# First attention layer: the twelfth tile's probabilities summed on TensorE instead of VectorE, and the keys' last third made one pair of tiles later

## The reference, cut to what matters

```python
def _L0_xattn_ref(hidden_q, kv_c, Wq, w_kc_q, w_kc_kv, W_qr, W_kr, Wo):
    q_hk = (hidden_q @ Wq.T).reshape(Bv, Sv, H, K)
    q_big = _apply_rope(jnp.einsum('bshk,hkq->bshq', q_hk, w_kc_q), ...)
    kv_r = _apply_rope(kv_c, sin_k[None], cos_k[None])
    q_r = jnp.einsum('bshq,hqr->bhsr', q_big, W_qr)
    k_r = jnp.einsum('bld,hdr->bhlr', kv_r, W_kr)
    scores = jnp.einsum('bhsr,bhlr->bhsl', q_r, k_r)
    attn = jax.nn.softmax(scores, axis=-1)
    ctx_c = jnp.einsum('bhsl,bld->bhsd', attn, kv_r)
    ...
x = x + _L0_xattn_ref(_layernorm(x, axis=-1), ctx_512, ...)
```

## Time and profile before

| | |
|---|---|
| median of three runs | 3072.91 us (3068.79 to 3073.55) |
| profiled execution | 3062.97 us, its span 3061.2 us, mean granted clock 0.944 |
| busy in the span | PE 2756.9 us (90%), DVE 1929.9 (63%), ACT 1131.7 (37%), POOL 1876.1 (61%) |
| first layer's attention | about 110 to 1425 us in the span |
| POOL's additions there, L1183 | 608 instructions, 804.8 us |
| DVE's `context`, L1325, in 180 to 1420 us | 28 with a `prob` operand, 51.9 us busy, 56.3 us of waiting for POOL ahead of them |

### The profile page before, as it was taken

The page is one execution under the profiler, slowest core; times in us unless marked ns, Lnnn a source line. Parts: engine busy times, 40 slices in busy tenths (PEclk is TensorE's granted clock), DMA queues, the critical chain, the costliest instruction groups (busy, mean ns, idle before and its releaser), DMA issues. The chain is left out here.

```text
span 3061.2 us, 43235 instructions
## 1 busy us (share of the span) xinstructions
PE 2756.9 (90%) x15928; PEld 1710.1 (56%) x15928; DVE 1929.9 (63%) x2342; ACT 1131.7 (37%) x1640; POOL 1876.1 (61%) x1239
## 2 busy tenths in 40 slices
PE   7688989989899989998789979999999999987898
PEld 6444545545445545454678855555555555545665
DVE  3576657665766666663666556665665765646664
ACT  3124441444134432443433224443444443433331
POOL 0469975999769976995200007877877877951111
PEclk8789999999999999999899988999999999997999
DMA  8333331333213331331000033323323323310000
GB/s 298 113 79 78 88 98 35 71 93 91 66 41 91 97 85 35 75 88 63 32 1 1 1 78 80 86 61 83 86 61 83 86 68 79 86 42 13 7 7 12
DMA packets 98841, 209.19 MB, mean 68 GB/s; under 512 B 30306, under 2 KB 74322, under 8 KB 91116
## 3 DMA queue, kind: packets, MB, share of 16 engines
q1 hardware_dynamic: 98636, 206.44, 26.4%
HBM read 135.36 MB, written 46.00 MB: 59 GB/s over the span
## 5 line engine op out<-in xcount | busy, mean ns | idle before, releaser
L1289 DVE TENSOR_REDUCE maxpart<-pair 112x2 f32<-112x1000 f32 x744 | 890.2, 1197 | 428.3 <-PE pair L978 427.2
L1118 ACT ACTIVATE prob<-wide 125x896 f32<-125x896 f32 x768 | 671.5, 918 | 723.0 <-PE wide L1004 619.8
L1183 POOL TENSOR_TENSOR sums<-sums,prob 125x448 f32<-125x448 f32 x544 | 708.6, 1324 | 45.9 <-POOL sums L1183 38.6
L1018 PE MATMUL single<-prob,kv 125*64 125x448 f32 x3072 | 692.1, 565 | 0.7 <-ACT prob L1118 0.7
L1186 POOL TENSOR_TENSOR sums<-sums,prob 125x896 f32<-125x896 f32 x284 | 615.0, 2165 | 113.4 <-ACT prob L1118 76.9
L999 PE MATMUL wide<-qhigh,kparts 64*125 64x448 f32 x3072 | 447.8, 369 | 1.8 <-ACT prob L1118 1.4
L978 PE MATMUL pair<-kparts,qhigh 64*112 64x500 f32 x1488 | 340.7, 454 | 82.0 <-DVE maxpart L1289 80.7
L1018 PEld LDWEIGHTS single<-prob,kv 125*64 125x64 f32 x3072 | 215.5, 139 | 264.2 <-issue 196.8
L978 PEld LDWEIGHTS pair<-kparts,qhigh 64*112 64x112 f32 x1488 | 131.6, 173 | 379.9 <-DVE maxpart L1289 244.1
L999 PEld LDWEIGHTS wide<-qhigh,kparts 64*125 64x125 f32 x3072 | 285.2, 185 | 60.0 <-issue 29.1
L1004 PE MATMUL wide<-shift,ones_row 64*125 64x448 f32 x1536 | 283.1, 364 | 0.5 <-DMA shift<-maxrow 0.5
(11 more groups left out here) (334 smaller groups left out, 4033.3 us busy)
## 6 DMA issues: line engine op xcount, KB each, us to landing
kparts<-keys_merged SPq DMA_DIRECT2D x64, 750.0 KB, 8.8
kparts<-kparts SPq DMA_DIRECT2D x96, 250.0 KB, 3.1
keys_merged<-kparts SPq DMA_DIRECT2D x32, 750.0 KB, 10.4
recip<-zrec_merged SPq DMA_DIRECT2D x124, 112.0 KB, 2.8
w_low_values<-w_merged SPq DMA_DIRECT2D x64, 192.0 KB, 2.4
raw<-in_ctx SPq DMA_DIRECT2D x32, 375.0 KB
values_merged<-kv SPq DMA_DIRECT2D x32, 375.0 KB
kv<-values_merged SPq DMA_DIRECT2D x32, 375.0 KB
```

Source lines behind the costliest of these rows:

```text
L1018: mm = pe.matmul(mix_acc[64 * half:64 * half + DC, 0:HQ], kv[:, b % 3, t, :], prob[:, (b * LT + t) % NPROB, half * HQ:(half + 1) * HQ], st ...
L1118: nc.scalar.activation(prob[:, n_ % NPROB, :].rearrange("p (a b) -> p a b", a=2), acc[0:LP, :, 0:HQ], ACT.Exp)\
L1183: nc.gpsimd.tensor_tensor(dst[:, cols], first_in[:, cols], prob[:, n_ % NPROB, cols], ALU.add)\
L1289: V.tensor_reduce(maxpart[:, b % 2, t:NMAX:4, third], acc[0:TQ, :, 0:LB], AX.X, ALU.max).then_inc(*R.signal_drained(kind, *key))
```

## The change: what it does

In the first layer, for the 28 batches in which POOL adds eleven tiles:

- DVE's `context` addition goes. A new step `last`, right behind the batch's last mix at `p == 0` of the next batch, multiplies tile 11's `prob` by the ones on PE into region 3 (`start=True, stop=False`).
- `norm`, at its old place at `p == 1`, multiplies `sum_pool` by the ones into the same accumulator (`start=False`). It waits for POOL's sums in place of DVE's. Region 3 is thus held from `last` on.
- ACT's reuse of tile 11's `prob` buffer waits for `last` (`last_summed`), and POOL's reuse of a `sum_pool` buffer for the `norm` two batches back.
- For the first seven batches of a group the last third of `keyT` moves from `p == 4` to `p == 5`, on PE, ACT, DVE and SP, with the DMAs behind it.

```diff
+def last_on_tensor(layer, b):
+    return layer == 0 and pool_tiles(layer, b) == POOL_TILES
...
+                if p == 5 and j < BG - 1 and b + 2 < NB:
+                    add("keyT", b + 2, 2, region=3)
                 if j or p:
                     add("mix", old[0], old[1])
                     add("mix", old[0], old[1] + 1)
                     if not p:
+                        add("last", b - 1)
                         add("context", b - 1)
...
-                if p == 4 and b + 2 < NB:
+                if p == 4 and j == BG - 1 and b + 2 < NB:
                     add("keyT", b + 2, 2, region=3)
...
+                elif kind == "last" and last_on_tensor(layer, key[0]):
+                    b, = key
+                    R.room(pe, "norm", b)
+                    pe.wait_ge(*R.drained("score", b, LT - 1))
+                    for half in range(2):
+                        mm = pe.matmul(region[3][64 * half:64 * half + DC, 0:HQ], c["ones"][0:LP, :],
+                                       prob[:, (b * LT + LT - 1) % NPROB, half * HQ:(half + 1) * HQ], start=True, stop=False)
+                    mm.then_inc(s["last_summed"], 1)
                 elif kind == "norm":
-                    pe.wait_ge(s["dve_sum"], vector_sums(layer, b + 1))
+                    summed = sum_dve
+                    if last_on_tensor(layer, b):
+                        pe.wait_ge(s["pool_half"], pool_sums(layer, b + 1))
+                        pe.wait_ge(s["pool_sum"], pool_sums(layer, b + 1))
+                        summed = sum_pool[:, b % 2, :]
+                    else:
+                        pe.wait_ge(s["dve_sum"], vector_sums(layer, b + 1))
...
+                        elif last_on_tensor(layer, bo):
+                            act.wait_ge(s["last_summed"], tensor_sums(layer, bo + 1))
...
+                            if b >= 2 and last_on_tensor(layer, b - 2):
+                                pool.wait_ge(*R.filled("norm", b - 2))
...
-                elif kind == "context":
+                elif kind == "context" and not last_on_tensor(layer, key[0]):
```

More of the change, by code:

```diff
@@ L63, in pool_sums, with tensor_sums @@
     return sum(pool_tiles(layer, i) - 1 for i in range(b))
+def last_on_tensor(layer, b):
+    return layer == 0 and pool_tiles(layer, b) == POOL_TILES
+def tensor_sums(layer, b):
+    return sum(last_on_tensor(layer, i) for i in range(b))
 def vector_sums(layer, b):
-    return sum(LT - pool_tiles(layer, i) for i in range(b))
+    return sum(0 if last_on_tensor(layer, i) else LT - pool_tiles(layer, i) for i in range(b))
 def query_pieces(layer, g):
@@ L569, in build_program @@
                "keys_moved_0", "keys_moved_1", "keys_moved_2", "values_moved_0", "values_moved_1", "values_moved_2", "w_high", "w_low", "qcos", "qsin", "qrot", "qhigh",
-               "maxneg", "premix", "mixed", "pool_half", "pool_sum", "dve_sum", "recip", "sums_packed", "packed_recip", "recip_stored", "recip_spread", "ctx_ready", "attn_half",
+               "maxneg", "premix", "mixed", "last_summed", "pool_half", "pool_sum", "dve_sum", "recip", "sums_packed", "packed_recip", "recip_stored", "recip_spread", "ctx_ready", "attn_half",
                "rank_step", "routed", "cw_zeroed", "cw_high", "e_high", "e_low", "gate_act", "hid_ready", "hid_high", "hid_low", "down_done",
@@ L1020, in _ @@
                     mm.then_inc(s["premix"], 1)
+                elif kind == "last" and last_on_tensor(layer, key[0]):
[6 more added lines that the diff above has]
+                    mm.then_inc(s["last_summed"], 1)
                 elif kind == "norm":
                     b, = key
-                    pe.wait_ge(s["dve_sum"], vector_sums(layer, b + 1))
+                    summed = sum_dve
[5 more added lines that the diff above has]
+                        pe.wait_ge(s["dve_sum"], vector_sums(layer, b + 1))
                     for half in range(2):
                         mm = pe.matmul(acc[64 * half:64 * half + DC, 0:HQ], c["ones"][0:LP, :],
-                                       sum_dve[:, half * HQ:(half + 1) * HQ], start=True, stop=True)
+                                       summed[:, half * HQ:(half + 1) * HQ], start=not last_on_tensor(layer, b), stop=True)
                     mm.then_inc(*R.signal_filled(kind, *key))
@@ L1171, in _ @@
                         if t == 1:
-                            if b >= 2:
+                            if b >= 2 and last_on_tensor(layer, b - 2):
+                                pool.wait_ge(*R.filled("norm", b - 2))
+                            elif b >= 2:
                                 pool.wait_ge(s["dve_sum"], vector_sums(layer, b - 1))
@@ L1298, in _ @@
                     b, t = key
-                    if t > pool_tiles(layer, b):
+                    if t > pool_tiles(layer, b) and not last_on_tensor(layer, b):
                         n_ = b * LT + t
```

## The result

The changed kernel takes 3033.41 us, the median of four runs (3030.49 to 3038.87); the kernel before, on the same chip, 3073.23 us (3068.79 to 3076.71). The profiled execution of the changed kernel took 3034.39 us, close to its median.

The account below looks back on a forecast made before the run. The prediction took POOL to pace the batch. The removed addition gives 24 x 0.84 = 20.2 us, all other terms 0, so 3072.91 - 20.2 = 3052.7 us, with a range from 3034 to 3074.

Parts of the forecast that it names:

- The bound: First layer's 24 batches: POOL paces the batch at 29.95 us; TensorE by itself needs 27.05 us.
- The addition that goes: VectorE's `context` addition holds up POOL's first two half additions; removing it gives back 0.84 us a batch, 20.2 us.
- The wait that moves: `norm` on TensorE now waits for POOL's sums, which are ready before TensorE comes to it; cost 0.
- The third that moves: Keys' last third, one pair later: same work, VectorE's stop there replaces the one at `context`; taken as 0.
- The product: New ones product on TensorE, 0.86 us a batch, hidden by its wait for POOL; cost 0, at most 20.6 us.
- The four additions at the last batch: VectorE's other four additions, one a group, where the group's last batch begins; their removal taken as 0.
- The sum: All terms together: 20.2 us off, giving 3052.7 us.
- More than forecast: Rival: remaining collisions fall well (rotation 0.40 instead of 1.42), POOL gets another 1.0 us a batch; 3029 us; chance 0.09.
- The lock goes elsewhere: Rival: VectorE's other two-input instructions' collisions with POOL are drawn anew, half the 0.84 lost; 3062.8 us; chance 0.20.
- TensorE becomes the pace, slower: Rival: moved third holds VectorE, TensorE stops and its clock falls; 31.2 us a batch, 3103 us; chance 0.08.
- Nothing moves: Rival: TensorE is the pace already, so the removed addition was hidden and the product isn't; 3073 us; chance 0.13.
- What would show it: Signs: POOL's first half additions 2.24 us, batch 29.1, no other idle, 28 products, `sums` only in last batches, `norm` unwaiting.

Follow-up runs that it names:

- e4: Changed kernel plus a VectorE addition of two SBUF inputs, result unused, where the removed addition stood, without waiting for POOL; 3042.42 us, ratio 0.9924 to the kernel before.
- e5: Changed kernel plus a VectorE maximum over one SBUF input, result unused, at the place of the removed addition; 3034.09 us, ratio 0.9892 to the kernel before.
- e1: Kernel before with only the keys' last third moved one pair later, VectorE still adding the twelfth tile; 3057.54 us, ratio 0.9967 to the kernel before.
- e2: Changed kernel with the keys' last third put back to its old place, TensorE still summing the twelfth tile; 3032.07 us, ratio 0.9883 to the kernel before.
- e6: Changed kernel without its new product, the twelfth tile left out of the softmax's sum; 3020.59 us, ratio 0.9848 to the kernel before.
- e9: Changed kernel with the eleventh tile's ones product on TensorE too and the keys' last third at its old place; 3016.60 us, ratio 0.9826 to the kernel before.
- e8: Changed kernel with the rotation's two cosine products moved directly behind its additions on VectorE, one piece instead of three; 3064.35 us, ratio 0.9989 to the kernel before.
- e7: Changed kernel with the eleventh tile's probabilities also summed by a ones product on TensorE, POOL adding nine tiles; 3023.41 us, ratio 0.9857 to the kernel before.

## Why the prediction was right in direction and too small

**The bound: right, with less room than it said.** POOL paced the batch, and relieving it shortened the batch.

**The addition that goes, 0.84 a batch: right in size, and the lock is shown.** The first additions went from 3.08 to 2.23-2.26 us, and e4 and e5 show that it is the second input. The rule of the Trainium skill ("SBUF — State Buffer", Who interferes with whom) gave an estimate of 1.08 a batch; the row's 0.84 was the one to take. That this by itself comes off the batch is not shown: a collision of 0.83 us, put back at another place (e4), cost 0.08 a batch in the trace.

**The wait that moves, taken as 0: right.** `norm` has no wait in the 24 batches.

**The third that moves, taken as 0: wrong alone, and right beside the product for a reason that the prediction did not give.** Alone (e1) it is worth 12.3 us in the 24 batches and 10 in all. The prediction looked only at what its wait might cost. It missed that the wait also sets where the scaled context, queued behind the subtraction, meets POOL: at one place in 21 of the 24 batches, where POOL loses 0.16 us instead of 0.61. In the changed kernel that is 0.45 of the 1.44 that POOL gets back a batch, the context's addition 0.84, and the remaining 0.15 is the net of the rest. But beside the product the held third also brings TensorE's stops and POOL's waits for exponentials, and e2, without it, is as fast: POOL works 6.2 us longer there and idles 9.6 less. The whole gain comes without the third.

**The product, taken as hidden: this term failed.** e6's trace prices it at 0.54 a batch. The working compared TensorE's time without its stops (27.9) with POOL's (29.1 us); but POOL's need fell further, to 28.4 (648.29 / 24 = 27.0 busy, and eight round trips of 0.17), and TensorE's stop for the maxima, 0.83 to 1.86 us, stayed. 27.9 and the stop are 28.7 to 29.8: there was no room. Had the product been free, the changed kernel would be at 3020 us by the traces, at about 3026 by the ratios.

**The four additions at the last batch, taken as 0: failed.** The working said that the new product takes more than the 0.74 us by which `norm` waited. It does, but it runs ahead, in time in which TensorE waits anyway. In three of four groups `norm` came 1.3 us sooner, and 0.8 later in the fourth. Of the 8.7 us that the layer gained outside the 24 batches this explains less than half; e1 gained 18.2 in the layer, 5.9 of it there as well. The rest stays open.

**The sum.** In the 24 batches 20.2 were forecast and 27.5 measured: 34.5 of POOL's time, less 7 more of its idle time. With 8.7 outside them it is 36.2. The timed gain was 40 us. That the time came out just at the end of the range is in part luck: POOL got back more than forecast, and the product's cost, taken as 0, ate some of it.

**The rivals.** "More than forecast" is what happened (3029 against 3033), but with another collision than the one it named: not the rotation, which still costs 0.9 to 1.5 us, but the scaled context. "The lock goes elsewhere" named the right mechanism and had the sign wrong. Its "drawn anew" is what e2 and e4 show. "TensorE becomes the pace, slower" is refuted: VectorE is held at the third, as that rival had it, but TensorE's stops got shorter at their longest (3.40 to 1.86), and the mean clock rose from 0.95 to 0.98. "Nothing moves" is refuted.

**What would show it.** Four of the signs came true: 2.24 us, 28 new products, no `sums` on VectorE but those of the last batches, `norm` without a wait in the paced batches. One did not, and the prediction had named it as what would prove it wrong: POOL has idle time besides the 0.17, 1.3 us in eight batches.

## What to carry to other kernels

Where two engines lock each other out, moving an instruction can change the collisions behind it; an edit priced at 0 because "it only moves" was worth 12.3 us alone in the 24 batches here, where the one that removes work was worth 30.9, and the two don't add up. Before a cost is called hidden by another engine's room, subtract that engine's waits that will stay, not only its busy time. When both engines are near full, it can pay to give work to the one that then runs without stops: e9, with two products, is faster than the changed kernel though it has more TensorE work.

## What the runs showed of the hardware that was not expected

- The lock takes from both sides, and which side pays depends on the order in which they meet. In e8 four operations of VectorE in a row took 1.01 + 2.82 = 3.83 us for some 2.1 of work, while POOL's two additions beside them took 3.19 + 2.66 for 4.48.
- A VectorE operation of 0.55 us, a cosine product, costs POOL 1.4 us: the addition at 660.32 above takes 3.62 instead of 2.24. It stands directly behind a maximum with one input. By the rows POOL did next to none of its work while that maximum ran. VectorE in the changed kernel there, and the second half of POOL's addition by itself:

```profile
660.16 1.20 DVE L1318 TENSOR_REDUCE maxpart<-pair 112x2 f32<-112x1000 f32 x1 [0.57 <-PE pair L989]
661.28 0.55 DVE L1233 TENSOR_TENSOR rope_c<-raw,cosk 125x384 f32<-125x384 f32 x1
```

```profile
662.79 1.14 POOL L1212 TENSOR_TENSOR sums<-sums,prob 125x448 f32<-125x448 f32 x1
```

  The first half thus lasted from 660.32 to about 662.8, 1.0 us beyond the product's end at 661.83. Of the 1.14 us that a half takes, less than 0.2 can have run before, in the 0.96 us from the addition's start to the product's. A maximum alone doesn't hold POOL: 233 half additions of these batches that meet nothing else of VectorE take 1.13 to 1.17 us. Why the product's lock reaches back is open.

- At the same busy time of TensorE (661.95 and 661.55 us in the 24 batches) and more work, the mean granted clock was 0.98 with one ones product a batch and 1.00 with two, where the stops for the maxima were never longer than 0.85 us (1.86 at 670.42 in the changed kernel). What e7 added to TensorE it got back by the clock.
